# Centring the key and query weights with a constant matrix on TensorE in a decoder layer

## What is computed

```python
qkv = jnp.einsum('bsh,oh->bso', x, w_qkv)        # x: already layer-normed
q, k, v = jnp.split(qkv, [H * D, (H + HKV) * D], axis=-1)
q = _layernorm(q, qn_g, qn_b)                    # over the 128 of each head
k = _layernorm(k, kn_g, kn_b)
# _layernorm(x, g, b): mu = mean(x); (x - mu) * rsqrt(mean((x - mu)**2) + EPS) * g + b
```

## Time and profile before

| | |
|---|---|
| median of 3 runs | 1552.28 us (1549.75 to 1555.59) |
| the profiled execution's own time | 1553.64 us |
| its span, first to last instruction | 1551.8 us |
| PE busy | 1380.3 us, 89% of the span |
| DVE, ACT, POOL busy | 861.3, 652.5 and 396.8 us |

### The profile page before, as it was taken

One profiled execution on the slowest core, in us unless ns is written; L12 is line 12 of the kernel. 1 busy time (PEld: TensorE's weight loads), 2 busy tenths in 40 slices (PEclk: granted clock), 3 DMA queues, 4 the chain that ended last, 5 costly groups with the idle time before them and its releaser, 6 DMA issues.

```text
span 1551.8 us, 31106 instructions
## 1 busy us (share of the span) xinstructions
PE 1380.3 (89%) x11264; PEld 877.3 (57%) x11264; DVE 861.3 (56%) x1887; ACT 652.5 (42%) x1447; POOL 396.8 (26%) x311
## 2 busy tenths in 40 slices
PE   2799999999999999798888989898989768999997
PEld 1456666666666556556566656566656534555554
DVE  7876676676766776534433333343333588534433
ACT  2433333333333333535555556555555612323322
POOL 5643434444343444111111111111111166000000
PEclk9799999999999999999999999999999979999999
DMA  8300000000000000211111111111110151000000
GB/s 264 106 1 0 0 0 0 0 0 0 0 0 0 0 0 32 89 61 41 40 39 39 39 39 39 39 40 60 57 39 21 56 217 54 23 1 21 0 22 22
DMA packets 22270, 58.33 MB, mean 38 GB/s; under 512 B 1262, under 2 KB 9454, under 8 KB 19026
## 3 DMA queue, kind: packets, MB, share of 16 engines
q1 hardware_dynamic: 22226, 57.74, 11.1%
HBM read 54.46 MB, written 3.28 MB: 37 GB/s over the span
## 4 chain that ended last, share of the span: by engine, by line
PE 67%; DVE 20%; issue 6%; ACT 4%; POOL 2%; DMA 1%; DVEq 0%; ACTq 0%; SPq 0%; POOLq 0%
PE A L1385 17%; PE A L1353 11%; PE C L1606 9%; PE A L1301 8%; PE C L1409 4%; PE B L1426 4%; PE C L1320 3%; PE A L1621 3%; PE B L1621 3%; DVE ssq L832 2%; PE B L1312 2%; DVE xn L905 1%; PE B L1394 1%; DVE ub L827 1%; ACT sq L508 1%
## 5 line engine op out<-in xcount | busy, mean ns | idle before, releaser
L1301 PE MATMUL A<-arena,xh 128*100 128x512 f16 x768 | 185.1, 385 | 21.5 <-DVE arena L1052 13.6
L1353 PE MATMUL A<-arena,stageb 128*100 128x512 f16 x768 | 176.0, 379 | 28.6 <-DVE stageb L878 27.9
L1385 PE MATMUL A<-wxh,arena 128*122 128x512 f16 x768 | 199.7, 383 | 0.0
L1606 PE MATMUL C<-arena 128*128 128x400 f16 x1024 | 188.2, 338 | 8.7 <-DVE arena L980 8.7
L424 POOL TENSOR_TENSOR arena<-arena,region 100x512 f32<-100x512 f32 (+1 forms) x64 | 69.2, 1110 | 483.4 <-DVE region L941 483.4
L401 POOL TENSOR_TENSOR region<-tb,ub 100x512 f32<-100x512 f32 x80 | 108.5, 1356 | 293.7 <-DVE ub L828 293.7
L585 ACT ACTIVATE arena<-C 122x1600 f32<-122x1600 f32 x96 | 144.5, 1506 | 36.6 <-PE C L1409 34.5
L1606 PEld LDWEIGHTS C<-arena 128*128 128x128 bf16 x1024 | 101.8, 100 | 85.2 <-issue 14.9
L1301 PEld LDWEIGHTS A<-arena,xh 128*100 128x100 f16 x768 | 95.2, 127 | 92.6 <-issue 20.0
L1353 PEld LDWEIGHTS A<-arena,stageb 128*100 128x100 f16 x768 | 92.8, 125 | 94.5 <-issue 34.5
L522 ACT ACTIVATE region<-C,negm 100x100 f32<-100x100 f32 x256 | 84.2, 347 | 147.3 <-DVE negm L867 147.3
(11 more groups left out here) (174 smaller groups left out, 2336.7 us busy)
## 6 DMA issues: line engine op xcount, KB each, us to landing
stageb<-in_wffn SPq DMA_DIRECT2D x16, 768.0 KB, 6.4
arena<-in_ctxt SPq DMA_DIRECT2D x16, 722.0 KB, 4.7
stageb<-in_wffn SPq DMA_DIRECT2D x8, 1024.0 KB, 4.8
arena<-in_wqkv SPq DMA_DIRECT2D x4, 1024.0 KB, 15.0
arena<-in_wffn SPq DMA_DIRECT2D x4, 1024.0 KB, 5.8
out_x<-xres SPq DMA_DIRECT2D x16, 200.0 KB
arena<-in_wx SPq DMA_DIRECT2D x3, 1024.0 KB, 7.0
xres<-in_x SPq DMA_DIRECT2D x1, 3000.0 KB
```

What stands on the lines that cost most here:

```text
L1301: ins = pe.matmul(A[j % 2][0:S, :], xp[:, k, :], wp[:, j, k, :], start=(n == 0), stop=(n == 11))
L1353: ins = pe.matmul(A[0][0:S, :], ap[:, h, :], wohl[:, g, part, h % 4, :], start=(n == 0), stop=(n == 47))
L1385: ins = pe.matmul(A[(par + n) % 2][0:rows, :], lhs, wp[:, 0 if n == 0 else 1 if n < 4 else 2, k, :], start=(i == 0), stop=(i == 11))
L1606: ins = pe.matmul(C[2 * (e % 2) + half][:, 0:UB * S], wf[:, 3 * (e // 4) + half, k, (e % 4) * 128:(e % 4 + 1) * 128], part[:, k, :], start ...
```

## The change

The sum, division and subtraction for pieces 0 to 4 go. In their place PE multiplies each 128 x 128 block of the weights by the constant matrix I - 1/128, which the constants now hold (128 columns more). For that the pieces come from memory in their natural layout, with a head's 128 rows on the partitions, so that the product comes out transposed as it is needed, and centred. It lands in the PSUM tile `C`, in two halves of 1024 columns; ACT makes the high half straight from there (`w_centred`) and DVE the low half (`w_centred_lo`). `centre(j)` on PE has 16 fp32 matmuls; before it writes a half of `C` it waits until DVE has read that half of the piece before (`d_cen`). Pieces 5 to 9 are made as before. The loads are reordered (row 0 of `x` is first, the gains and biases come after piece 0, rows 1 and 2 of `x` after piece 5, and the other 13 rows at the end), DVE makes `x_lo(0)` ahead of the rotary tables, and `w_lo(6)` and `w_lo(7)` stand after the second and the fourth `z_back`.

```diff
+    c[:, C_CEN:C_CEN + D] = np.eye(D) - 1.0 / D
...
         def _(sp):
-            sp.dma_start(cst[:], consts).then_inc(ld_c, 16)
-            sp.dma_start(gain[:], gains).then_inc(ld_c, 16)
-            sp.dma_start(bcol[:], bcols).then_inc(ld_c, 16)
             xt = x.rearrange("(b p) f -> p b f", b=NB)
             sp.dma_start(xres[:, 0, :], xt[:, 0, :]).then_inc(ld_x0, 16)
+            sp.dma_start(cst[:], consts).then_inc(ld_c, 16)
             for j in range(10):
                 if j >= 8:
 
-                    sp.wait_ge(a_whi, j - 7)
-                    sp.wait_ge(d_wlo, j - 7)
+                    sp.wait_ge(pe_cen, 2 * (j - 7))
                 dst, loaded, _ = staged(j)
                 sp.dma_start(dst, wqkv[:, j] if j < 6 else wo[:, j - 6]).then_inc(loaded, 16)
+                if j == 0:
+                    sp.dma_start(gain[:], gains).then_inc(ld_g, 16)
+                    sp.dma_start(bcol[:], bcols).then_inc(ld_g, 16)
                 if j == 5:
-                    sp.dma_start(xres[:, 1:NB, :], xt[:, 1:NB, :]).then_inc(ld_x, 16)
+                    sp.dma_start(xres[:, 1:3, :], xt[:, 1:3, :]).then_inc(ld_x1, 16)
+            sp.dma_start(xres[:, 3:NB, :], xt[:, 3:NB, :]).then_inc(ld_x, 16)
...
         def _(pool):
-            pool.tensor_copy(idh[:], cst[:, C_ID:C_ID + 128]).then_inc(g_setup, 1)
-            for j in range(5):
-
-                pool.wait_ge(d_wmean, j + 1)
-                w = staged(j)[0].rearrange("p k (h d) -> p (k h) d", h=4)
-                pool.tensor_tensor(w, w, wmean[:, j].unsqueeze(2).broadcast_to([128, KT * 4, D]),
-                                   ALU.subtract).then_inc(g_wcen, 1)
...
         def _(act):
+            def w_centred(j, half):
+
+                act.wait_ge(pe_cen, 2 * j + half + 1)
+                act.activation(wqh[:, j, 2 * half:2 * half + 2],
+                               Call[:, half * 1024:half * 1024 + 1024].rearrange("p (k n) -> p k n", k=2),
+                               ACT.Copy, scale=SW).then_inc(a_cen, 1)
...
+            for half in range(2):
+                w_centred(0, half)
             for j in range(5):
+                if j < 4:
+                    for half in range(2):
+                        w_centred(j + 1, half)
+                else:
+                    w_hi(5)
                 square(0, j)
-                w_hi(j + 3)
             v_of(0)
             x_hi(1)
-            for j in range(8, 10):
+            for j in range(6, 10):
                 w_hi(j)
...
         def _(dve):
-            def w_mean(j):
+            def w_centred_lo(j, half):
+
+                dve.wait_ge(a_cen, 2 * j + half + 1)
+                dve.scalar_tensor_tensor(wql[:, j, 2 * half:2 * half + 2].rearrange("p k n -> p (k n)"),
+                                         Call[:, half * 1024:half * 1024 + 1024], SW,
+                                         wqh[:, j, 2 * half:2 * half + 2].rearrange("p k n -> p (k n)"),
+                                         ALU.mult, ALU.subtract).then_inc(d_cen, 1)
...
-            for j in range(2, 5):
-                w_mean(j)
-                w_lo(j - 2)
-            proj(0, 0)
-            for j in range(3, 6):
-                w_lo(j)
-                proj(0, j - 2)
-            proj(0, 4)
-            dve.wait_ge(ld_x, 16)
+            for j in range(5):
+                if j < 4:
+                    for half in range(2):
+                        w_centred_lo(j + 1, half)
+                else:
+                    w_lo(5)
+                proj(0, j)
+            dve.wait_ge(ld_x1, 16)
             row_stats(1, ssq[:, 20:21])
             head_norm(0)
             normed(1, rstd[:, 20:21])
-            w_lo(6)
             x_lo(1)
-            w_lo(7)
             for g in range(5):
                 z_back(0, g)
+                if g == 1 or g == 3:
+                    w_lo(6 + g // 2)
...
         def _(pe):
+            def centre(j):
+
+                src, loaded, n = staged(j)
+                pe.wait_ge(loaded, n)
+                for half in range(2):
+                    if j > 0:
+                        pe.wait_ge(d_cen, 2 * (j - 1) + half + 1)
+                    for k in (2 * half, 2 * half + 1):
+                        for h in range(4):
+                            ins = pe.matmul(C[k][:, h * D:(h + 1) * D], src[:, h, k * 128:(k + 1) * 128],
+                                            cst[:, C_CEN:C_CEN + D], start=True, stop=True)
+                    ins.then_inc(pe_cen, 1)
...
             x_turn(0)
-            for j in range(6):
-                pe.wait_ge(a_whi, j + 1)
-                pe.wait_ge(d_wlo, j + 1)
+            centre(0)
+            for j in range(5):
+                if j < 4:
+                    centre(j + 1)
+                pe.wait_ge(a_cen, 2 * j + 2)
+                pe.wait_ge(d_cen, 2 * j + 2)
                 project(0, j)
+            pe.wait_ge(a_whi, 1)
+            pe.wait_ge(d_wlo, 1)
+            project(0, 5)
```

More of the change, by code:

```diff
@@ L240, in build @@
         ld_c = sem("ld_c")
+        ld_g = sem("ld_g")
+        ld_x1 = sem("ld_x1")
         ld_x0 = sem("ld_x0")
@@ L244, in build @@
         ld_wx = [sem(f"ld_wx{j}") for j in range(3)]
-        g_setup = sem("g_setup")
         d_tab = sem("d_tab")
-        d_wmean, g_wcen, a_whi, d_wlo = sem("d_wmean"), sem("g_wcen"), sem("a_whi"), sem("d_wlo")
+        pe_cen, a_cen, d_cen, a_whi, d_wlo = sem("pe_cen"), sem("a_cen"), sem("d_cen"), sem("a_whi"), sem("d_wlo")
         d_step = sem("d_step")
@@ L609, in _ @@
             x_hi(0)
-            for j in range(3):
-                w_hi(j)
+            for half in range(2):
+                w_centred(0, half)
             for j in range(5):
+                if j < 4:
[3 more added lines that the diff above has]
+                    w_hi(5)
                 square(0, j)
-                w_hi(j + 3)
             v_of(0)
             x_hi(1)
-            for j in range(8, 10):
+            for j in range(6, 10):
                 w_hi(j)
@@ L1027, in _ @@
             normed(0, rs1[:, 0:1])
-            dve.wait_ge(ld_c, 48)
+            x_lo(0)
+            dve.wait_ge(ld_c, 16)
+            dve.wait_ge(ld_g, 32)
             for w, g in ((0, 2), (1, 0)):
@@ L1037, in _ @@
             dve.wait_ge(d_tab, 6)
[L1039 to L1044 removed]
+            def w_centred_lo(j, half):
[4 more added lines that the diff above has]
+                                         ALU.mult, ALU.subtract).then_inc(d_cen, 1)
             def w_lo(j):
[L1048 removed]
+                dve.wait_ge(a_whi, j - 4)
                 dst, hi = (wql[:, j], wqh[:, j]) if j < 6 else (
@@ L1055, in w_lo @@
                    .then_inc(d_wlo, 1)
-            w_mean(0)
-            x_lo(0)
-            w_mean(1)
-            for j in range(2, 5):
-                w_mean(j)
-                w_lo(j - 2)
-            proj(0, 0)
-            for j in range(3, 6):
-                w_lo(j)
-                proj(0, j - 2)
-            proj(0, 4)
-            dve.wait_ge(ld_x, 16)
+            for half in range(2):
+                w_centred_lo(0, half)
+            for j in range(5):
[6 more added lines that the diff above has]
+            dve.wait_ge(ld_x1, 16)
             row_stats(1, ssq[:, 20:21])
@@ L1669 @@
     q, k, v = wqkv[:H * D], wqkv[H * D:(H + HKV) * D], wqkv[(H + HKV) * D:]
-    wqkv = tiles(np.concatenate([k, q, v]))
-    wqkv = wqkv.reshape(128, KT, 6, 512).transpose(0, 2, 1, 3)
+    heads = np.concatenate([k, q]).reshape(5, 4, D, DM).transpose(2, 0, 1, 3)
+    wqkv = np.concatenate([heads, tiles(v)[:, None]], 1)
     wo = tiles(f["L0_attn_w_o"]).reshape(128, 4, 4, DM)
```

38 lines of the change are left out of this document (14 added, 24 removed).

## The result

The changed kernel takes **1583.35 us** (median of 4 runs, 1581.74 to 1588.27) against 1553.1 us for the kernel before (4 runs beside them, 1549.75 to 1555.59): 1.0198 times as long, with an interval of 1.0177 to 1.0219. It is slower by 30 us, and 1544.0 was predicted, with 1549 as the upper end. The profiled execution of the changed kernel took 1588.27 us with a span of 1586.5 us, against 1553.64 and 1551.8.

What follows compares the result with a forecast made beforehand. DVE and POOL were taken to bound the setup, PE the turns behind it. Gains of 6.25 us up to row 1's statistics and 2.1 after, less 0.05, made 8.3: 1544.0 us from the median 1552.28, range 1541 to 1549.

Steps and rivals of the forecast that it cites:

- The rival on the slower side: Setup: PE at clock 0.50 (12.4 us a piece, 1569.7 us) or matmuls and loads one after another (1559.2); chance 0.05.
- Row 0 of `x`: Start of setup: first in the load queue, it lands after 4.2 us, between 3.6 and 6.9, instead of 6.21.
- rival 2: Start of setup: row 0 of `x` again takes 6.21 us, PE starts at 11.9; shift 6.3, 1546.0 us; chance 0.08.
- Start: Start of setup: PE free at 9.2 us, piece 0 landed and centring begun at 9.8, with 9.2 and 10.6 as ends.
- rival 3: Start of setup: clock rises early or piece 0 lands at 9.2; shift about 10 us, 1542.3 us; chance 0.06.
- A record of 0.113 us: PE's centring in the setup: each 128-column fp32 matmul record takes 0.113 us, sized from `scores`, 3.62 us a piece.
- Rival 1: PE's centring: a record costs 0.138 us as in `attend`, 4.4 us a piece; shift 5.2, 1547.1 us; chance 0.09.
- the serial rival: PE's centring: matmuls and weight loads one behind the other, 0.226 us a record; loss 7 us, 1559.2; within a 0.05 chance.
- the rule that was cited for it: Trainium skill, for PE: a weight load runs beside matmuls only when they use other rows of the array.
- `w_lo(5)`: End of setup's weight phase: on DVE ahead of `proj(4)`, until 46.85 us; the statistics of row 1 then start at 48.7.
- From the statistics to `w_lo(8)`: Rest of setup: 3.7 us to the reciprocal roots, then 15.0 instead of 17.1 to `w_lo(8)`; 2.1 us won, less 0.05.
- The sentence on what makes it wrong: Signs of failure: PE waiting for `d_cen` every piece, a record over 0.125 us, or a changed first-turn length from `w_lo(8)`.

Runs made afterwards that it cites:

- experiment 3: Changed kernel with 155 hidden padding instructions, loads back in the old order: 1547.33 us; kernel before with new loads and moved low halves, without PE centring: 1552.57 us.
- spread_early_w5: Changed kernel with padding under PE's waits, piece 5's high and low halves made ahead of `proj(0, 1)` instead of `proj(0, 4)`: 1543.58 us, 0.9948 of the kernel before.
- experiment 2: Changed kernel with 155 waiting PE instructions spread over places where PE idles, the loop again in 7 blocks: 1544.43 us, 0.9945 of the kernel before.
- after_pad40: Changed kernel with 40 semaphore increments that nobody waits for at the head of PE's text, loop in 8 blocks: 1604.67 us, 1.0327 of the kernel before.

## Why the prediction was wrong, and where it was right

**The step that failed** is in its first paragraph: "What the setup gains moves everything behind it forward once, since no load is near in time there". Everything behind the setup was taken as unchanged, because its text is. It had one kind of load in view, that of data. So a term of the sum, what the change does to the turns behind the setup, stood at nothing. The program itself is loaded too, and the 323 instructions that the setup got longer moved the cross attention's loop from seven blocks into eight. A loss of 41.2 us there, 37.3 of it behind the jumps back, stands against a gain of 8.1 in the setup. The rival on the slower side put its mechanism into the setup (PE at half pace) and gave it 0.05; the rate of PE in the setup was right, and the loss had another cause. None of the rivals held this one, so the range could not. Part of it lay open: the page of before has the code queue (28 packets), and the diff shows how many matmuls PE's text gets more. With the loop's length they would have raised the question. How many blocks stay loaded no row of the kernel before tells; that took the experiments.

**The forecast of the setup**, by its terms:

- *Row 0 of `x`*: 4.2 was taken, 3.81 measured. It went as taken; the new order of the loads is worth 2.4 us (experiment 3), near the 2 us that rival 2 gave it.
- *Start*: piece 0 was forecast for 9.8 and centring began at 8.83. The first three projections ended 0.9 to 1.0 us before their forecast (22.2, 28.4, 34.5 for 23.1, 29.3, 35.5). That is the early end of rival 3.
- *A record of 0.113 us*: right. 32 take 3.73 us with their tail, and the doubled centring gives 3.58 for 32, 0.112. Rival 1 (0.138) is out; its own sum doesn't come out either, since the 3.9 us that it names would leave 4.4 of the 8.3, and it says 5.2. The weight loads took 3.76 us beside the 3.73 us of matmuls, so the serial rival is out too, and with it, for this shape, the rule that was cited for it.
- *Halves*: ACT 1.02 (1.03 forecast), DVE 1.23 (1.21).
- *PE as the bound, period 6.2*: right, 6.16, with a granted clock of 1.00.
- *`w_lo(5)`*: sized at 2.28, measured 3.05 (43.43 to 46.48), with POOL at work beside it for the first 0.9 us; in spread_early_w5 it stood at 28.27 us with POOL idle and took 2.29. That ate most of the microsecond from the start: statistics at 48.26 for 48.7.
- *From the statistics to `w_lo(8)`*: 18.7 us forecast (48.7 to 67.4), 19.45 measured. `w_lo(6)` took 2.68 us beside the last `z_of`, for which 0.05 had been left; it cost 0.4. PE's scores took 5.35 us at the lower level, from 60.67, for 60.1 to 65.4.
- *The sum*: 67.5 forecast for `w_lo(8)`, 67.71 measured; 8.3 us of shift forecast, 8.1 measured.

With the loop back in seven blocks (experiment 2) the total is 1544.43 us, where 1544.0 was forecast. So the sum for what it covered held. That its errors of a microsecond cancelled was luck, and so is the match of the totals to 0.4 us: the kernels before lay 1.3 us apart (1552.28 and 1553.55), and the gain was 9.1 where 8.3 was forecast.

**The sentence on what makes it wrong** named the first turn's length. It did not change (7.9 us ahead at the next turn's scores). It looked next to the setup, and the reloading began some 700 us behind it. To name one turn of each later loop as well would have cost a line.

## What to carry to other kernels

When an edit changes how many instructions an engine has, compare the code queue of the two profiles and find the longest loop of that engine that comes after: its cost can depend on where it starts, and the text of the loop shows nothing of it. Here a loop of 1676 PE instructions was free where it ended 66 or more short of the end of its seventh block of 256, and cost 6.2 us at each jump back where, by the count, it reached one instruction into the eighth. A wait for "issue" at the same place in every turn with the clock at half behind it is how it looks. Padding under a wait that is there anyway, or a shorter loop body, puts it back, and what an edit elsewhere is worth can be read only where both kernels have their loops loaded for good.

## What was not expected of the hardware

- This loop on PE stayed loaded up to about seven blocks of 16 KB and was then loaded again after every jump back: 9 packets and 6.2 us each time (37.3 us over six). The jump itself took 3.60 to 3.84 us instead of 0.21; the rest is the clock, at 0.50 for 3.5 us and at 0.87 to 0.89 around it. The Trainium skill (Advanced Engine Details and Errata, ISA Cache) gives TensorE 128 KB, which is eight blocks, and says that there are only 2 cache lines. The first figure is one block above what stayed here; the second, if it is meant for TensorE too, is contradicted by the single packet in 435 us of looping.
- Between the two (41 and 16 instructions short of the end of the seventh block) two of the six jumps back paid in each profiled execution, 8.8 to 9.3 us together, and the runs of one kernel lie up to 15 us apart. A packet that starts 3.7 or 3.8 us ahead of the jump marks those that pay; why it starts in some turns only is open.
- With the same number of packets a turn, nine, one offset had one stall a turn and another two (after 607.3 us, after_pad40 625.8).
- Two short dips of the clock ahead of the loop (granted 0.56 and 0.66 in after) cost 3.4 to 3.9 us in three of the profiled executions and don't occur in the others. They are enough to hide a gain of 3 us in the setup.
- A semaphore increment that does nothing else takes PE 0.15 us when nothing covers it (110 of them: 16.8 us).
